# Second edge stage of a two-layer graph network: maps with edges on the output rows, weighting moved to VectorE, weighting and totals seven sub-batches behind, and the group's difference behind the weighing

## The reference, cut to what matters

```python
ms = src_s[edge_src] + dst_s[edge_dst]; mv = src_v[edge_src] + dst_v[edge_dst]
w1, w2, w3, w4, w5 = split(w)                # w: a small network of edge_scalars
ds = concat([w1 * ms, w4 * (mv . Y1)])       # 96 scalars
dv = concat([(w2*ms) Y1, w3 * mv, w5 * cross(mv, Y1)])
ls, lv = _eq_lin(ds, dv, lin_ws, lin_bs, lin_wv)
a = einsum('ehk,hk->eh', _smooth_leaky(ls[:, :64]), alpha_dot)   # 8 heads
a = exp(a - segment_max(a, edge_dst)[edge_dst]); a = a / segment_sum(a, edge_dst)
ns = segment_sum(vs * a, edge_dst)           # vs: 8 scalars of each head
nv = segment_sum(vv * a, edge_dst)           # vv: 4 vectors of each head
```

## Time and profile before

| | |
|---|---|
| median of three runs | 9831.51 us |
| profiled execution, its time | 9813.87 us |
| its span, first to last instruction | 9812.0 us |
| granted TensorE clock, mean | 0.944 |
| busy over the span: TensorE, VectorE, GpSimd, ScalarE | 85%, 79%, 75%, 50% |

### The profile page before, as it was taken

The page is one execution under the profiler, slowest core; times in us unless marked ns, Lnnn a source line. Parts: engine busy times, 40 slices in busy tenths (PEclk is TensorE's granted clock), DMA queues, the critical chain, the costliest instruction groups (busy, mean ns, idle before and its releaser), DMA issues. The chain is left out here.

```text
span 9812.0 us, 193495 instructions
## 1 busy us (share of the span) xinstructions
PE 8373.1 (85%) x35878; PEld 5079.2 (52%) x35878; DVE 7735.9 (79%) x14864; ACT 4874.4 (50%) x9073; POOL 7372.6 (75%) x4571
## 2 busy tenths in 40 slices
PE   0788888888888869999985999999999999998588
PEld 0444444444444422222222777777777777777233
DVE  3177777777777768888886999999999999998465
ACT  0176666666666631121121555555555555555355
POOL 4378888888888878778774888888888888886331
PEclk9599999999999989999997999999999999999799
DMA  5578888888888877778773666666666666665222
GB/s 208 180 161 167 167 168 166 167 167 167 167 167 167 167 213 275 267 271 282 264 270 109 136 137 144 137 143 137 144 138 144 138 142 137 144 137 122 59 70 52
DMA packets 1235170, 1618.04 MB, mean 165 GB/s; under 512 B 222610, under 2 KB 1010589, under 8 KB 1178973
## 3 DMA queue, kind: packets, MB, share of 16 engines
q1 hardware_dynamic: 758950, 1273.86, 40.0%
q0 software_dynamic: 475584, 338.58, 27.1%
HBM read 1533.79 MB, written 444.07 MB: 202 GB/s over the span
## 5 line engine op out<-in xcount | busy, mean ns | idle before, releaser
L1952 POOL DMA_INDIRECT e_m<-TS,e_at x1568 | 2631.8, 1678 | 583.7 <-issue 461.4
L442 POOL DMA_INDIRECT sums<-e_total,e_place x1568 | 2506.9, 1599 | 565.9 <-DMA sums<-e_total,e_place 314.5
L579 PE MATMUL ps<-e_win,e_pick 128*128 128x448 f32 x3136 | 1325.8, 568 | 165.0 <-DVE e_u L476 97.0
L579 PEld LDWEIGHTS ps<-e_win,e_pick 128*128 128x128 f32 x3136 | 612.5, 201 | 921.6 <-issue 864.1
L2275 ACT ACTIVATE e_dT<-ps 128x512 f32<-128x512 f32 x1176 | 660.0, 596 | 495.5 <-PE ps L2149 340.1
L2275 ACT ACTIVATE e_oT<-ps 128x512 f32<-128x512 f32 x784 | 468.9, 598 | 615.1 <-PE ps L2177 373.2
L742 DVE SCALAR_TENSOR_TENSOR r_y<-ps,w_rb,r_rstd 128x512 f32<-128x512 f32 x394 | 295.6, 750 | 579.9 <-issue 533.2
L1096 POOL TENSOR_TENSOR n_zv<-n_zv,n_ast 128x1536 f32<-128x1536 f32 x200 | 703.6, 3518 | 36.6 <-DMA n_zv<-in_x_groups 22.5
L1936 POOL TENSOR_TENSOR e_val<-e_val 128x640 f32<-128x640 f32 x392 | 670.9, 1712 | 61.9 <-ACT e_val L2252 61.9
L2018 DVE TENSOR_TENSOR e_q<-e_row,dstI 128x512 f32<-128x512 int32 x392 | 704.2, 1796 | 13.3 <-PE ps L2163 13.3
L711 PE MATMUL ps<-r_sq,w_avg 128*128 128x512 f32 x788 | 458.1, 666 | 277.4 <-issue 277.4
(11 more groups left out here) (448 smaller groups left out, 19299.8 us busy)
## 6 DMA issues: line engine op xcount, KB each, us to landing
e_win<-T SPq DMA_DIRECT2D x1568, 168.0 KB
n_z<-in_x_groups SPq DMA_DIRECT2D x400, 512.0 KB
n_zv<-in_x_groups SPq DMA_DIRECT2D x800, 192.0 KB
TOT<-e_tot SPq DMA_DIRECT2D x392, 352.0 KB, 2.6
e_row<-in_src_rows SPq DMA_DIRECT2D x98, 1024.0 KB
e_local<-LR SPq DMA_DIRECT2D x196, 512.0 KB
e_row<-in_dst_rows SPq DMA_DIRECT2D x98, 1024.0 KB
e_win<-TD SPq DMA_DIRECT2D x1568, 60.0 KB
```

Source lines behind the costliest of these rows:

```text
L442: pool.indirect_dma_start(sums[c], bass.IndirectOffsetOnAxis(ap=place[:, r % 4, c:c + 1], axis=0), total[:, r % 4, c, 0:MSG0], None, compu ...
L579: pe.matmul(g[:, c, :], pick[:, p, R * c:R * c + R], win[:, s, c, :], start=True, stop=True).then_inc(spread, 1)
L1952: pool.indirect_dma_start(m_[:, r % 4, c, :], None, TS, bass.IndirectOffsetOnAxis(ap=at[:, gp, col:col + 1], axis=0), compute_op=ALU.add). ...
```

## The change

The maps change operands. Each 128 edges of `dT` become the stationary operand and the weights the moving one, so the result has edges on rows at once. `map_scalars` writes bank 4 in four matmuls, `map_vectors` writes bank 5 in eight, and `turn_back`, its 3136 transposes and the two copies to `oT` go. Alpha and scalars now lie in one bank, vectors in the other, and each has its own condition for being overwritten: `map_scalars(i)` waits for ScalarE's copies and for VectorE's first operation of `results(i-1)`, and `map_vectors(i)` for `freed`. `weighted` goes to the start of VectorE's iteration, seven behind. `totals` goes to seven behind. On TensorE `tops_down` goes ahead of `turn(i, 0)`, the first half of `totals` behind `turn(i, 2)`, and the second half behind `map_vectors`. `shift` goes behind `weigh`. `members`, with its wait on L2017, isn't touched.

```diff
             @block.gpsimd
-                        if not i.before(8):
-                            weighted(i, 8)
             @block.vector
                 def results(i):
                     dve.wait_ge(outs, i.n(2, 2))
+                    dve.scalar_tensor_tensor(out=silu[:, p], in0=silu[:, p], scalar=1.5, in1=alpha4, ...
+                                             ).then_inc(silued, 1)
+                    dve.wait_ge(mapped, i.n(2, 2))
                     for x in range(3): ...            # by_y
-                    dve.scalar_tensor_tensor(...).then_inc(silued, 1)
                 def body(t):
+                        if not i.before(7):
+                            weighted(i)
                         if more:
                             sums(after)
...
+                        if more:
+                            weigh(after)
                         if r % 4 == 1 and not i.before(5):
                             shift(i)
-                        if more:
-                            weigh(after)
                         if not i.before(5):
                             members(i)
             @block.tensor
                 def totals(i, half):
-                    j = i.r - 6
+                    j = i.r - 7
                 def map_scalars(i):
-                    pe.wait_ge(kept, i.n(5, 2))
-                    pe.matmul(ps[:, bank(i, 5), :], W["la"][:]..., dT[:, 0, :], start=True, stop=True
-                              ).then_inc(turned, 1)
+                    pe.wait_ge(kept, i.n(3, 1))
+                    if not i.before(1):
+                        pe.wait_ge(outs, i.n(2))
+                        pe.wait_ge(silued, i.n(2, -1))
+                    for c in range(GT):
+                        last = pe.matmul(scalar_out4[:, c], dT[:, 0, R * c:R * c + R],
+                                         W["la"][:].rearrange("u a h x -> u (a h x)"), start=True, stop=True)
+                    last.then_inc(mapped, 1)
                 def map_vectors(i):
+                    pe.wait_ge(kept, i.n(3, 3))
+                        pe.wait_ge(freed, i.n(1))
                     for c in range(GT):
-                        last = pe.transpose(out4[:, c, 128 * j:128 * j + 128], oT[:, j, R * c:R * c + R], I[:])
+                        pe.matmul(vector_out4[:, c], dT[:, 1, R * c:R * c + R], W["lb"][:]..., start=True, stop=False)
+                        last = pe.matmul(vector_out4[:, c], dT[:, 2, R * c:R * c + R], W["lc"][:]..., start=False, stop=True)
                     last.then_inc(mapped, 1)
                 def body(t):
                         if i.plus(3).within():
                             spread_out(i.plus(3), 0, ...)
-                        if not i.before(1):
-                            turn_back(i.plus(-1), 0)
                             spread_out(i.plus(3), 1, ...)
-                        if not i.before(1):
-                            turn_back(i.plus(-1), 1)
                             weights(after)
+                        if r % 4 == 1 and not i.before(5):
+                            tops_down(i)
                         pe.wait_ge(d_ready, i.n(1, 1))
                         turn(i, 0)
                         turn(i, 1)
-                        if not i.before(6):
-                            totals(i, 0)
+                        map_scalars(i)
                         turn(i, 2)
-                        if r % 4 == 1 and not i.before(5):
-                            tops_down(i)
-                        map_scalars(i)
-                        if not i.before(6):
+                        if not i.before(7):
+                            totals(i, 0)
+                        map_vectors(i)
+                        if not i.before(7):
                             totals(i, 1)
-                        map_vectors(i)
             @block.scalar
                 def body(t):
+                        if r % 4 == 2 and not i.before(6):
+                            weigh_up(i.plus(-1))
                         keep(i, 0)
                         keep(i, 1)
-                        keep_totals(i, 0)
                         keep(i, 2)
-                        keep(i, 3)
-                        keep_totals(i, 1)
-                        keep(i, 4)
+                        results(i)
+                        keep_totals(i, 0)
+                        keep_totals(i, 1)
```

More of the change, by code:

```diff
@@ L2109, in _ @@
                 for r in range(5):
+                    weighted(At(PASSES, r))
                     members(At(PASSES, r))
+                for r in range(5, 7):
+                    weighted(At(PASSES, r))
             @block.tensor
@@ L2152, in totals @@
                 def totals(i, half):
-                    j = i.r - 6
+                    j = i.r - 7
                     slot = j % STEPS
                     gate(pe, k)
-                    pe.wait_ge(u_ready, i.n(1, 1, 6))
+                    pe.wait_ge(u_ready, i.n(1, 1, 7))
                     gate(pe, k)
-                    pe.wait_ge(q_ready, i.n(1, 1, 6))
-                    if not (i.before(7) and half == 0):
+                    pe.wait_ge(q_ready, i.n(1, 1, 7))
+                    if not (i.before(8) and half == 0):
                         gate(pe, k)
-                        pe.wait_ge(totkept, i.n(2, half, 6))
+                        pe.wait_ge(totkept, i.n(2, half, 7))
                     for c in (2 * half, 2 * half + 1):
@@ L2168, in map_scalars @@
                     gate(pe, k)
-                    pe.wait_ge(kept, i.n(5, 2))
-                    pe.matmul(ps[:, bank(i, 5), :], W["la"][:].rearrange("u a h x -> u (a h x)"), dT[:, 0, :], start=True, stop=True
-                              ).then_inc(turned, 1)
+                    pe.wait_ge(kept, i.n(3, 1))
+                    if not i.before(1):
+                        gate(pe, k)
+                        pe.wait_ge(outs, i.n(2))
+                        gate(pe, k)
+                        pe.wait_ge(silued, i.n(2, -1))
[3 more added lines that the diff above has]
+                    last.then_inc(mapped, 1)
                 def map_vectors(i):
                     gate(pe, k)
[L2175 to L2183, removed]
+                    pe.wait_ge(kept, i.n(3, 3))
+                    if not i.before(1):
                         gate(pe, k)
@@ L2186, in turn_back @@
                     for c in range(GT):
-                        last = pe.transpose(out4[:, c, 128 * j:128 * j + 128], oT[:, j, R * c:R * c + R], I[:])
+                        pe.matmul(vector_out4[:, c], dT[:, 1, R * c:R * c + R], W["lb"][:].rearrange("u h x -> u (h x)"),
+                                  start=True, stop=False)
+                        last = pe.matmul(vector_out4[:, c], dT[:, 2, R * c:R * c + R],
+                                         W["lc"][:].rearrange("u h x -> u (h x)"), start=False, stop=True)
                     last.then_inc(mapped, 1)
@@ L2306, in body @@
                             keep_far(i.plus(3), 1, far2(i, 1))
-                        if not i.before(1):
-                            results(i.plus(-1))
+                        if r % 4 == 2 and not i.before(6):
+                            weigh_up(i.plus(-1))
                         keep(i, 0)
                         keep(i, 1)
-                        if not i.before(6):
+                        keep(i, 2)
+                        results(i)
+                        if not i.before(7):
                             keep_totals(i, 0)
-                        keep(i, 2)
-                        keep(i, 3)
-                        if not i.before(6):
                             keep_totals(i, 1)
-                        if r % 4 == 1 and not i.before(5):
-                            weigh_up(i)
-                        keep(i, 4)
                 act.preload_act_table_set("exp_and_others")
@@ L2325, in _ @@
                 passes(act, body)
-                results(At(PASSES - 1, STEPS - 1))
                 weigh_up(At(PASSES, 1))
-                for r in range(6):
+                for r in range(7):
                     for half in range(2):
```

81 lines of the change are left out of this document (37 added, 44 removed).

## The result

The changed kernel takes 10623.55 us, the median of four runs (10615.14 to 10633.33), against 9826.76 us for the kernel before. The ratio is 1.081, with a 95% interval from 1.0789 to 1.083. The forecast was 10680 us. The experiments were timed later, and the kernel before then took 9795.32 us (four buffers, totals early, first operation, filler) and 9798.69 us (the other four).

What follows compares the result with a forecast made beforehand. A ring of waits between VectorE and TensorE, 10.0 us a sub-batch, was taken as the new bound: 9813.9 + 650 (ring) + 200 (clock) = 10664, median 18 us above, 10680. Range 10270 to 10970.

Steps and rivals of the forecast that it cites:

- ring: Comparison, first operation of `results`, both maps, second half of `totals`, next comparison: 10.0 us, against 8.14 for VectorE alone.
- VectorE's leg of the ring: Comparison 0.60, weighting 0.73, `sums` 2.63, `selections` 0.39, first operation of `results` 0.41: in all 4.76 us.
- TensorE's leg with all handovers: `map_scalars`, transposes, ScalarE's copy, `map_vectors`, second half of `totals`: 4.57 us, plus 0.65 for handovers, weight-load leads and VectorE's register operation.
- The scan's sub-batch: `tops_down` ahead of `turn(i, 0)` waits for the scan's end, so `map_scalars` starts at about 7.3: 12.5 us, twice a pass.
- The end of a pass: VectorE's branch, 4.1 us in its queue, stands behind the waiting comparison: 3.9 us more, on the ring.
- The sum: 6 x 10.0 + 2 x 12.5 + 3.9 = 88.9 us a pass; +650 us, +200 for the clock: 10680.
- The clock: TensorE at half speed after idle gaps: 1.4 us three times a pass, 4.2 us, +200 us; rival without it 20 in 100.
- The maps' loads: Rival, 4 in 100: 24 weight loads not hidden behind matmuls, +2.6 us in each ring, +1000 us, so 11680.
- The signs: Idle 1.5 to 2 us ahead of the comparison, comparison 0.68, VectorE near 75%, clock below 0.99, pass near 93 us.
- `shift` at no cost: `shift` behind `weigh` lies in time the comparison waits for: no cost; without that cover up to 0.42 us twice a pass.
- The rival on the other side: Ring doesn't hold, VectorE is the bound: 72.0 us a pass, 9670; needs TensorE's leg under 3.4 us; 9 in 100.

Runs made afterwards that it cites:

- four buffers: Changed kernel with four buffers for q instead of two, so the comparison waits for totals of i-9, not i-7: 9937.3 us, ratio 1.0139.
- totals early: Changed kernel with each half of `totals` moved ahead of the map it stood behind, ScalarE's copies moved to match: 9644.9 us, ratio 0.9842.
- first operation: Changed kernel with VectorE's first operation of `results(i-1)` moved ahead of `sums`: 10277.66 us, ratio 1.0488.
- filler: Changed kernel with useless TensorE transposes ahead of `weights`, 20 in a scan's sub-batch and 30 behind the branch: 10392.38 us, ratio 1.0603.
- the other four: Tops-back run 1.0624, weighting-back run 1.0238, totals early plus four buffers 0.9861, old maps' run 0.9842.
- tops-back run: Changed kernel with `tops_down` put back behind TensorE's second turn: 10410.48 us, ratio 1.0624.
- old maps' run: Kernel before, with weighting on VectorE and `totals` and stores seven behind; maps, `turn_back`, `tops_down` and `shift` as they were: 9645.06 us, ratio 0.9842.
- weighting-back run: The totals early kernel with the weighting moved back from VectorE to GpSimd, behind its gathers: 10033.12 us, ratio 1.0238.

## Why the prediction was right

The forecast was that a ring which no busy share shows would replace VectorE's own time as the bound. The terms, one by one:

- VectorE's leg of the ring: 4.76 worked out, 4.79 measured. Its parts err both ways: the weighting was put at 0.73, and from its start to the next operation are 7083.0 - 7082.2, about 0.74.
- TensorE's leg with all handovers: 4.57 + 0.65 = 5.22 against 5.11. The ring is 9.90 to 10.04 by the sub-batch's place in the pass (means over 45 passes of the distance between comparisons, as in all such figures here), against 10.0.
- The scan's sub-batch: 12.5 and 1.4 for the clock, 13.9 in all, against 14.15 and 14.38. The cause was right, and the tops-back run shows it. The step that was short is the way from the scan's end to `map_scalars`. Worked out from 5.61 to 7.3, it runs from 5.68 to 7.74. That is 2.06 us where I had 1.69 for the tops, a turn of 0.60, a copy of 0.60 and the handovers. In the rows the turn starts 0.37 after the scan's end, at 7006.95, and the map 1.69 after that, at 7008.64, where turn and copy alone are 1.2. And 1.4 was too little for the clock in the second scan's sub-batch, which gained 1.9 in the filler run.
- The end of a pass: 3.9 on top of the ring and 1.4 for the clock, 15.3 in all, against 13.77 on average. This is the term that was mis-sized. The branch's wait in the queue is now 2.8 us (6068.3 - 6065.5), not the 4.1 of the earlier trace rows. The comparison and the weighting start 3.20 apart instead of 0.60, so the surplus is 2.6. With it TensorE's idle time at the end of a pass was too long, over 5 us against 4.19.
- The sum: 93.1 us a pass forecast (88.9 and 4.2), 92.16 measured. The two scans were too low by 0.7 in all, the end of the pass too high by 1.5, the five others too high by 0.15. The 0.95 us, times 48.1 passes, are 46 of the 56 us by which 10680 was too high. That the sum came out within 1% is in part luck, since the two larger errors have opposite signs.
- The clock: 4.2 us a pass put down, 4.2 given back by the filler. The mechanism is shown; that the figures agree is luck in part, since the three places gave 1.3, 0.9 and 1.9 and some drops were left. Both forecast gaps are there in the rows, with 3.27 and 4.19 us of idle time ahead of them.
- The maps' loads: `map_vectors` goes from 7022.15 to 7024.03 in 16 pieces, 0.12 each with the first, 0.11 between the later ones, as the earlier trace rows had it. The rival of 11680 is out. The rule of the Trainium skill (TensorE: Matmul & The Clock Gate, Part 3), that a load only overlaps matmuls of other row groups, isn't borne out here when taken alone: each of these pieces loads all 128 rows anew, and at 0.11 apart nothing comes on top. The same part also lets a load that goes to a background weight buffer run ahead of matmuls; no run here can tell whether that is what happens.
- The signs: idle time ahead of the comparison 1.66 to 1.80 in ordinary sub-batches, comparison 0.69, VectorE 2317.81 / 3100 = 75%, clock 0.92. All as written. The idle time at the end of a pass was put near 4 us and is 2.51, from the same error as the branch.
- `shift` at no cost: not tried by itself. The order of the old maps' run, with `shift` in its old place, gives the same pass as the totals-early run within 0.2 us, which speaks for it. Neither run has the ring, though, so for the changed kernel it stays open.

The rival on the other side was right in its price, but its condition doesn't hold for this order. With no ring a pass was worked out as 72.0 us and the time as 9670. The totals-early run has 72.49 and 9644.9. There too errors of opposite sign cancel in part. The sub-batch behind the branch takes 10.4 us where 11.0 was worked out, and the five ordinary ones take 8.15 to 8.63 where it was 8.14. Its condition, a TensorE leg under 3.4 us, isn't met by the diff's order, where the leg is 5.11. It is met once the second half of `totals` stands ahead of `map_vectors`, as in the totals-early run: there an L2014 ends at 7048.48 us and that half at 7051.67, 3.2 us later.

Three expectations after the result were too simple. In the four-buffers run I took VectorE for the next bound and hadn't added up TensorE's own order (8.98 us). In the first-operation run I missed the second ring, through `map_vectors` (9.17 us). In the weighting-back run I let only the comparison and the first operation be held, and in fact it is whichever operation on SBUF alone stands beside the weighting.

## What to carry to other kernels

When an operation of one engine is made to wait for work of the same iteration that an operation of another engine stands in front of, look for the way back. Follow both waits until they close, and add the legs up. If the ring is longer than the busiest engine's sub-batch, it is the bound, and no busy share tells of it before. A depth of seven doesn't help if the producer does its part late in the same iteration; moving that part ahead of what waits was free here, and should be tried before more buffers. And after a bound is removed, add up the next one on each engine in its written order, since TensorE's 8.98 us were as easy to read as VectorE's 8.14.

## What the runs showed of the hardware

- VectorE's queue waits at the loop's branch, from its branch to its next instruction, and for how long differs between kernels and from pass to pass: 3.8 to 4.3 us before (4.1 in the earlier trace rows), 2.8 to 3.1 here, 2.8 to 3.6 in the run with the old maps. ScalarE's and GpSimd's queues show 0.1 to 0.2 at the same branch. SyncE's, like VectorE's, is long, 3.3 us. What sets it wasn't settled.

```profile
L316 POOLq COMPARE_BRANCH  x2: 53/53/53, 7037.9 to 7130.4; - x2
L316 POOLq MOVE  x2: 29/29/29, 7038.1 to 7130.5; - x2
...
L316 SPq COMPARE_BRANCH  x1: 54/54/54, 7080.1 to 7080.1; - x1
...
L316 SPq MOVE  x1: 41/41/41, 7083.4 to 7083.4; - x1
```

- Idle gaps of 3 to 4 us ahead of TensorE's work cost it twice here, once as idle time and once as a lower clock afterwards (3.27 and 4.19 us of idle time, then 0.71 and 0.59). Filling them with work that nobody needs gave 4.2 us a pass back, 203 us in all.
- Each of the two pieces of an fp32 matmul of 128 columns with a fresh 128x128 stationary operand takes 0.11 us in a row of its like. A piece of 512 columns takes 0.43, so the cost of a column is about the same.
- GpSimd's weighting holds VectorE's operations on SBUF alone (L1981 from 0.28 to 2.63 us, L2065 from 0.24 to 1.42 on average), while L2027, which reads PSUM, keeps its 0.41.
